# Expert layers: lists for the tokens in two rounds, and half of the results summed in the loop

## The reference

```python
x = x + attn_a(layernorm(x))   # differential attention, 16 heads
x = x + ffn(layernorm(x))      # experts, first time
x = x + attn_b(layernorm(x))   # attention with decay, a scan over the sequence
x = x + ffn(layernorm(x))      # experts, second time
```

```python
scores = softmax(xf @ router_w.T)
topk_scores, topk_ids = top_k(scores, 2)
topk_scores = topk_scores / topk_scores.sum(-1, keepdims=True)
for each expert e:
    h = silu(xf @ w_gate[e]) * (xf @ w_up[e])     # 128 -> 512
    out += weight_of_e * (h @ w_down[e])          # 512 -> 128
```

## Time and profile before

| | us |
|---|---|
| median of 3 runs (1086.36 to 1089.39) | 1087.95 |
| span of the profiled execution | 1143.6 |
| PE busy in it | 992.5 (87%) |
| PEld busy | 675.0 (59%) |
| DVE busy | 751.2 (66%) |
| ACT busy | 744.4 (65%) |
| POOL busy | 438.1 (38%) |

### The profile page before, as it was taken

How to read it: one execution, slowest core, us unless ns; L and a number is a source line. 1 busy time by engine, 2 the same in 40 slices (tenths; PEclk the granted TensorE clock), 3 DMA queues, 4 the chain that set the end, 5 groups by cost and what they waited for, 6 DMA issues and landing times. The chain is left out here.

```text
span 1143.6 us, 27230 instructions
## 1 busy us (share of the span) xinstructions
PE 992.5 (87%) x10390; PEld 675.0 (59%) x10390; DVE 751.2 (66%) x1507; ACT 744.4 (65%) x1507; POOL 438.1 (38%) x580
## 2 busy tenths in 40 slices
PE   5889999999999989747888978999999997688883
PEld 3333333333333335637888866878878876587883
DVE  6789999999999988872222265676666666422223
ACT  4658888888888877344444457767777765544443
POOL 3742112211222111325555334555555542455541
PEclk9879999999999999869999989999999999699997
DMA  2333111111111100611113122202114310211113
GB/s 70 96 114 98 30 32 52 34 30 30 36 52 30 30 2 2 221 44 38 38 37 110 30 75 98 75 38 75 76 75 149 111 39 2 63 38 36 38 34 124
DMA packets 42150, 68.67 MB, mean 60 GB/s; under 512 B 10088, under 2 KB 21096, under 8 KB 40104
## 3 DMA queue, kind: packets, MB, share of 16 engines
q1 hardware_dynamic: 33848, 54.07, 14.4%
q0 software_dynamic: 4992, 10.23, 3.2%
q10 hardware_dynamic: 3184, 2.63, 0.7%
HBM read 51.79 MB, written 14.68 MB: 58 GB/s over the span
## 5 line engine op out<-in xcount | busy, mean ns | idle before, releaser
L803 ACT ACTIVATE PB<-S 128x512 f32<-128x512 f32 x576 | 307.9, 597 | 71.6 <-PE S L609 66.8
L915 DVE TENSOR_REDUCE mx<-S 128x2 f32<-128x1024 f32 (+1 forms) x192 | 207.6, 1128 | 8.6 <-PE S L595 8.6
L871 POOL TENSOR_SCALAR_AFFINE_SELECT PB<-PB 128x512 f32<-128x512 f32 x128 | 79.0, 635 | 307.2 <-ACT PB L803 307.1
L1452 DVE TENSOR_TENSOR m_hs<-m_gs,m_UP 128x512 f32<-128x512 f32 x78 | 53.7, 688 | 213.2 <-ACT m_gs L1322 171.7
L644 PE MATMUL PV<-PB,VP 128*32 128x256 f32 (+2 forms) x2432 | 177.7, 379 | 0.0
L609 PE MATMUL S<-W 50*128 50x512 bf16 (+3 forms) x768 | 123.9, 328 | 4.9 <-ACT PB L803 4.2
L1250 PE MATMUL m_GP<-m_xt,m_wgu 128*128 128x128 f32 x624 | 89.3, 288 | 42.0 <-ACT m_xt L1318 38.7
L1197 POOL DMA_INDIRECT yd_rows<-m_ys,m_target x78 | 76.7, 983 | 115.5 <-DVE m_ys L1459 106.5
L1318 ACT ACTIVATE m_xt<-m_XT 128x128 f32<-128x128 f32 x78 | 21.6, 277 | 147.0 <-PE m_XT L1241 74.3
L1250 PEld LDWEIGHTS m_GP<-m_xt,m_wgu 128*128 128x128 f32 x624 | 79.7, 200 | 47.4 <-issue 47.4
L595 PE MATMUL S<-W 48*128 48x512 bf16 (+3 forms) x640 | 94.5, 326 | 13.6 <-DVE mx L911 4.9
(11 more groups left out here) (344 smaller groups left out, 1879.2 us busy)
## 6 DMA issues: line engine op xcount, KB each, us to landing
d_LQ<-l_rows SPq DMA_DIRECT2D x15, 1024.0 KB, 4.9
W<-qk_parts SPq DMA_DIRECT2D x210, 32.0 KB
qk_parts<-OT SPq DMA_DIRECT2D x24, 256.0 KB, 3.0
W<-qk_parts SPq DMA_DIRECT2D x30, 96.0 KB
W<-in_L_ffn_w_gate SPq DMA_DIRECT2D x1, 2048.0 KB, 9.4
W<-in_L_ffn_w_up SPq DMA_DIRECT2D x1, 2048.0 KB, 14.4
xn_rows<-m_XN SPq DMA_DIRECT2D x8, 256.0 KB, 2.3
W<-in_L_ffn_w_gate SPq DMA_DIRECT2D x2, 1024.0 KB, 5.4
```

The lines of the kernel that those rows point to most:

```text
L803: nc.scalar.activation(PB[:, j % NPB, :], S2[:, j % 3, :], ACT.Exp, scale=SC).then_inc(exp_done, 1)
L871: nc.gpsimd.affine_select(out=tri, in_=tri, compare_op=ALU.is_ge, fill=0.0, base=0, pattern=[[0, U], [1, P]], channel_multiplier=-1).then_ ...
L915: nc.vector.reduce_max(mx[:, g % 2, c, :, heads[0], qb], S1[:, b, :, 0:w], AX.X)\
```

## The change

The slots are ordered by sequence. First come the full slots that the first sequence's tokens alone fill, expert by expert, then for each expert a slot with the rest of them, filled up with tokens of the second sequence; these are at most FIRST = 8 * 2 + 7 = 23 slots. What is left of the second sequence follows, in slots by expert again. SLOTS stays 39.

The lists are made in two rounds, one for each sequence's tiles. The first needs two rounds of marks (23 slots wide) in place of four, and eight of its slots are gathered at once (EARLY = 8). The second round's counts stand on PE behind the first's, its bounds on DVE ahead of the slots, and the rest of it between the slots of DVE's queue, behind the gate of slot s and in front of the copy of slot s - 1. PE's products of the second round, 16 matmuls, stand behind the down matmuls of slot 3. POOL gathers nothing more until the scatter of slot 4, then two slots a scatter until it is nine ahead. The normalised rows of the second sequence are made on DVE in slot 3. In the first layer, the statistics of eight tiles move behind the first sources.

Once the first 23 slots are scattered, SP fetches the first sequence's results to GA, and DVE adds them, two tiles at a time, in slots 27, 29, 31 and 33; m2 stores these two quarters early. Behind the last slot two quarters are left of four. In m1 the moments of the first two quarters are taken in slots 32 and 36, and the front of `decay_attention` is arranged anew: its first rows need no sums.

RC and IV of the second round have PSUM banks of their own. Of the new functions, `first_bounds` has six linked steps (each waits for the one before), `second_bounds` five, `positions` seven; `mark_places` is one round of marks as before. The diff, cut to its core:

```diff
+def list_products(nc, IV, place_oh, marks, k, start, stop):
+    planes = 3 if k else 2
+    slots = marks.shape[3]
+    for i in range(8):
+        last = nc.tensor.matmul(IV[:, 0:planes * slots].rearrange("p (a s) -> p a s", a=planes), place_oh[:, k, :, i],
+                                marks[:, k, 0:planes, :, i], start=(start and i == 0), stop=(stop and i == 7))
...
+def first_bounds(nc, chain, lists, tmp, RC):
...
+def second_bounds(nc, chain, lists, tmp, RC):
...
+def positions(nc, chain, lists, tmp, RC, base, bound, OH):
...
+def mark_places(nc, chain, tmp, marks, place_oh, slot_no, lane_no, tile_no, iop, k, placed):
...
+def other_experts(nc, chain, lists, sef, early, etab_ready):
+    chain.link(nc.vector.tensor_tensor(sover[:, :, 2 * E:], lists["ios"][:].unsqueeze(2).to_broadcast([1, SLOTS, E]),
+                                       lists["late_ends"][0:1, 1:].unsqueeze(1).to_broadcast([1, SLOTS, E]), ALU.is_ge))
+    chain.link(nc.vector.reduce_sum(sef[:], sover[:], AX.X))
+    for k in (E - 1, 2 * E - 1):
+        chain.link(nc.vector.scalar_tensor_tensor(out=sef[:], in0=sover[:, :, k], scalar=-float(E), in1=sef[:], op0=ALU.mult,
...
+    EARLY = 8
+    FIRST = HT * 2 + E - 1
+    SUMS = FIRST + 4
...
+        def gathers_upto(s):
+            return EARLY if s < 4 else min(EARLY + 1 + 2 * (s - 4), s + 9, SLOTS)
...
             def _(sp):
+                for q in range(2):
+                    rows_out(q, xn_ready, TQ * q + TQ)
+                for q in range(2):
+                    rows_out(2 + q, xn_late, TQ * q + TQ)
+                all_stored(sp, FIRST)
+                for q in range(2):
+                    for k in range(2):
+                        sp.dma_start(GA[:, q, k], result_rows(k, q)).then_inc(first_gathered[q][k], 16)
...
             def _(pool):
+                for s in range(EARLY):
                     gather(s)
                 pool.wait_ge(targeted, 1)
+                issued = EARLY
                 for s in range(SLOTS):
+                    if s == EARLY:
+                        pool.wait_ge(targeted, 2)
                     scatter(s)
+                    if issued == EARLY and gathers_upto(s) > EARLY:
+                        pool.wait_ge(xn_stored[1], 16 * 2)
+                        pool.wait_ge(sourced, 2)
+                    for g in range(issued, gathers_upto(s)):
+                        gather(g)
+                    issued = gathers_upto(s)
...
             def _(pe):
+                first_counts(nc, RCA, route).then_inc(rca_done, 1)
+                second_counts(nc, RCB, route).then_inc(rcb_done, 1)
+                products(IVA, place_a, marks_a, 0)
...
                     down(s, e)
+                    if s == 3:
+                        products(IVB, place_b, marks_b, 2)
...
             def _(dve):
+                for k in (1, 0):
+                    mark_places(nc, chain, tmp, marks_a, place_a, slot_no[:, 0:FIRST], lane_no[:], tile_no[:, 0],
+                                lists["iop"][:, 0:1], k, placed)
...
+                make_sources(nc, chain, lists, token, 0, EARLY, sourced)
+                first_experts(nc, chain, lists, sef, EARLY, etab_ready)
+                if statistics_done < NT:
+                    moments(statistics_done, NT)
+                make_targets(nc, chain, lists, row, empty, 0, EARLY, targeted)
+                if statistics_done < NT:
+                    scale(2, statistics_done, NT, False)
+                    distances()
+                dve.wait_ge(rcb_done, 1)
+                second_bounds(nc, chain, lists, tmp, RCB)
...
                 for s in range(SLOTS):
                     gate(s)
+                    if s == 0:
+                        positions(nc, chain, lists, tmp, RCB, lists["rest"][:], lists["whole"][:], OH[:, :, HT:])
+                    elif s in (1, 2):
+                        marks_of_second(2 - s)
+                    elif s == 3:
+                        late_rows()
+                    elif s == 5:
+                        other_experts(nc, chain, lists, sef, EARLY, etab_ready)
+                    elif s == 6:
+                        make_targets(nc, chain, lists, row, empty, EARLY, SLOTS, targeted)
+                    elif s == 7:
+                        weights()
+                    elif s in range(SUMS, SUMS + HT, 2):
+                        early_sums(s - SUMS)
+                    elif follow is not None and s in (SUMS + TQ + 1, SUMS + HT + 1):
+                        early_moments(s - SUMS - TQ - 1)
                     if s:
                         y_copy(s - 1)
+                    if s == 4:
+                        other_lists()
...
@@ decay_attention, ACT
-                weigh_results(0)
-                weigh_results(1)
+                deviations(slice(0, 2 * TQ), 0)
+                rows(0)
                 weigh_results(2)
...
@@ decay_attention, DVE
+                row_scales(0)
+                row_scales(1)
+                add_results(2)
+                row_moments(2)
+                add_results(3)
+                row_scales(2)
+                row_moments(3)
```

More of the change, by code:

```diff
@@ new lines, in second_bounds @@
+def second_bounds(nc, chain, lists, tmp, RC):
+    E, HT = Router.E, Router.NT // 2
+    n = RC[:, HT * E:(HT + 1) * E]
+    over, late, ends = tmp["over"], lists["late"], lists["late_ends"]
+    chain.link(nc.vector.tensor_tensor(over[:], n.unsqueeze(2).to_broadcast([P, E, 2 * HT]),
+                                       lists["edges"][:, HT:].unsqueeze(1).to_broadcast([P, E, 2 * HT]), ALU.is_gt))
+    chain.link(nc.vector.reduce_sum(late[:, 1:], over[:], AX.X))
+    chain.link(nc.vector.tensor_tensor(late[:, 1:], late[:, 1:], lists["counts"][:, 1], ALU.subtract))
+    chain.link(nc.vector.tensor_tensor_scan(out=ends[:], data0=lists["ones_f"][:, 0:E + 1], data1=late[:], initial=0.0,
+                                            op0=ALU.mult, op1=ALU.add))
+    chain.link(nc.vector.tensor_tensor(lists["jump"][:], ends[:, 0:E], lists["past"][:], ALU.subtract))
@@ L1079, in moe @@
     FK = FF // P
+    HT = NT // 2
     NTOK, ROWS = NT * P, 2 * NT * P
@@ L1111, in moe @@
         wts = sb("wts", [P, 2, NT]) if follow is None else follow["wts"]
[L1112 to L1119, removed]
+        marks_a, marks_b = sb("marks_a", [P, 2, 3, FIRST, 8], BF16), sb("marks_b", [P, 2, 3, SLOTS, 8], BF16)
+        place_a, place_b = (sb(k, [P, 2, P, 8], BF16) for k in ("place_a", "place_b"))
+        sef = sb("sef", [1, SLOTS])
+        token, row, empty = (sb(k, [P, SLOTS]) for k in ("token", "row", "empty"))
+        etab, iv, source, target = (lists[k] for k in ("etab", "iv", "source", "target"))
         xs, xt = sb("xs", [P, XB, P]), sb("xt", [P, 2, P])
@@ L1224, in _ @@
-                counts()
-                order = [c for c in range(PC) if c >= PC // 2] + [c for c in range(PC) if c < PC // 2]
-                for m, c in enumerate(order):
-                    pe.wait_ge(placed, m + 1)
-                    planes = 3 if c >= PC // 2 else 2
-                    for i in range(PI):
-                        last = nc.tensor.matmul(IV[:, 0:planes * SLOTS].rearrange("p (a s) -> p a s", a=planes),
-                                                place_oh[:, c, :, i], marks[:, c, 0:planes, :, i],
-                                                start=(m == 0 and i == 0), stop=(m == PC - 1 and i == PI - 1))
@@ L1442, in _, with late_rows @@
[L1442 to L1447 removed]
+                def late_rows():
+                    for t in range(HT, NT):
+                        nc.vector.tensor_scalar(XN[:, t], X[:, t], mv[:, t, 0:1], rstd[:, t:t + 1], ALU.subtract, ALU.mult)\
+                          .then_inc(xn_late, 1)
```

431 lines of the change are left out of this document (270 added, 161 removed).

## The result

The changed kernel takes 1104.01 us (median of 4 runs, 1103.07 to 1107.59), the kernel before 1088.67 beside it: a ratio of 1.0138, interval 1.0104 to 1.0172. It is slower by 15.3 us, where 4.1 were forecast, and lies 7 us above the range.

A forecast was written before the change was run, and what follows sets the result against it. PE was taken to bound the slots, at a floor of 2.79 us each, holes left out. Slot costs of 17.1 less gains of 13.0 gave +4.1, so the median 1087.95 would become 1092.0 us, range 1080 to 1097.

The forecast's parts named there:

- price of the slots: Both loops over expert slots: inserted work costs 8.3 us per layer, twice 16.6, with the first layer's moments 17.1.
- marks: Slots, on DVE: two rounds of marks for the second sequence, 1.40 each, cost 1.3 us per layer.
- products: Slots, on PE: the second round's 16 matmuls cost 1.6 us per layer, bounds 1.43 and 2.87.
- experts and ninth gather: Slots: the other experts on DVE cost 1.4 us, the ninth gather behind the fifth scatter 0.8, per layer.
- early sums: Late slots, on DVE: four pairs of sums, each 1.2 us with a wait, cost 4 x 0.45 = 1.8 per layer.
- moments: First layer's slots, on DVE: 1.25 us twice, one between slots already delayed, cost 0.5.
- Holes, half or all: Rivals: timed loops have holes hiding half of DVE's price (1086.0 us, chance 0.28) or all (1079.8, chance 0.17).
- First front: Ahead of the first layer's slots: -1.6 us, limited by ACT's order; bounds -1.0 and -4.1.
- Second front: Ahead of the second layer's slots: fewer rounds of marks give -3.4 us, from -2.8 to -3.9.
- The decay attention: Its front: sums and moments of two quarters done beforehand, last quarter transposed earlier, -4.1 us, from -3 to -5.
- POOL held by DVE: Rival, slots: DVE's new work delays POOL's transfers, 1096.2 us; chance 0.10, shared with slot 27 late.
- The signs: Changed kernel: first gather at 11 to 13 us, later weights' copy, keys within 5, two tail quarters, PE waits in named slots.

The follow-up runs named there:

- third experiment: Changed kernel with the copies and multiplications in the first bounds written as two-input DVE operations; 1098.73 us, ratio 1.0102.
- fourth experiment: Changed kernel with the early sums one tile to a slot, slots 27 to 34, first-layer moments in slots 35 and 37; 1100.14 us, ratio 1.0103.
- first experiment: Changed kernel with DVE's copy of the slot before right behind the gate, the inserted work behind that copy; 1085.53 us, ratio 0.9958.
- second profile of before: The kernel before, unchanged, profiled once more; one time of 1088.79 us, loops 104.93 and 104.90.
- first recording: The kernel before, unchanged, in the profile the prediction read; span 1143.6 us with 54.2 us of holes in its two loops.

## Why the prediction was wrong

The direction was right, the bound too: PE in the slots, and the holes were rightly left out. The step that failed is the price of the slots, 17.1 where 28.2 were measured: products and early sums were priced too low, the delay of the ninth gather behind the experts too, and a fall of the clock was put at nothing. Against the steps of before (2.57 at first, 2.79, 1.95 at last), term by term:

| per layer, us | predicted | first layer | second layer |
|---|---|---|---|
| marks | 1.3 | 1.4 | 1.2 |
| late rows | 1.4 | 1.45 | 1.45 |
| products | 1.6 | 2.9 | 2.85 |
| clock behind them | 0 | 1.6 | 0 |
| experts and ninth gather | 2.2 | 3.3 | 3.25 |
| early sums | 1.8 | 3.4 | 4.2 |
| moments | 0.5 | 0.9 | - |

- **Products.** I named both ends, 1.43 and 2.87, and took 1.6, by the slot's own matmuls. It is the other end. In the kernel before, the sixteen of 117 columns took 3.44 at a granted clock of 0.50, and the sixteen of 78 behind them 2.56 (line L1231 by window again):

```profile
978.34:980.90 2.56, 2.53 (x17) 2.16 (x15) 0.50 0.00 0
```

So eight and eight are 3.00 at 0.50 (not 2.87: the narrow ones are not faster in proportion), and they took 3.04 and 3.02 at 1.00. Their pace comes from the spaced operand and not from the clock; with adjacent columns 1.12 are left. The Trainium skill ("SBUF — State Buffer", section "Door 1: The DMA port swizzle") states a penalty for each access that goes to a new 16-byte line; the 1.9 us between the two layouts agree. The fall of the clock behind the products (1.6) wasn't in the sum at all. It is not in every execution: the same products in the profiles of the third and fourth experiment had none behind them.
- **Sums.** The work was rightly sized (1.26 for four products), and I counted what exceeds a slack of 0.75. A stop costs PE 0.3 more here than it lasts, and the slack is smaller, 0.64: 0.54 late where 0.45 was counted. 0.86 in place of 0.45, four times in each layer. In the second layer two of these steps had 0.3 and 0.5 more beside a store of the output; no run separates that.
- **Experts and ninth gather.** DVE's experts (0.47, 1.12, 0.50, 0.17) held the copy, for which PE stood 1.47, thereby the fifth scatter, and behind it the ninth gather; I priced the two links singly. Placed behind the copy, 1.34 and 1.24 are left, and one slot earlier nothing.
- **Marks**: right by luck. I set 0.65 for each of two rounds. The first made a step of 4.21 and 4.06, 1.4 and 1.3 too long: in the first layer PE got its copy 0.96 late and paid 1.43. The second cost 0.06 and 0.07 (steps of 2.85 and 2.86), since behind the stop DVE is ahead of PE: its copy at 524.37 is done before the down matmuls at 525.58. **Late rows**: right. **Moments**: 0.9 for 0.5, all of it in slot 36; those between delayed slots cost nothing, as I had it.
- What I took as given in each of these terms was that the work stands ahead of the copy. That was true of the diff, and so a right premise for the time; but the profile had it in one line that it need not: DVE idle 1.90 in front of each gate. The first experiment shows this place to be worth 15.5 of the 28.2, or some more, since its profile has one fall of the clock more.

**What was gained.** Tail: -3.9 for -3.9. First front: -1.8 for -1.6, by the order on ACT that was named (the weights' copy, from 510.83 on, stands ahead of the transpose's copy, for which PE waits 2.03). Second front: -2.6 for -3.4; the stall of the third experiment, 0.9 by its first gate, is the difference (a slip is small beside it: four rounds of 1.40 less two of 1.15 are 3.30, not 3.35). The decay attention: more than -4.1. Its first keys and last quarter, in the changed kernel, whose stage begins at 648.87, and then in the second profile of before, where it begins at 630.14:

```profile
653.54 1.95 PE L1849 MATMUL d_PA<-d_WK,d_xc 128*128 128x512 f32 x4 [0.50 <-POOL d_xc L2300]
...
662.57 0.60 PE L1897 MATMUL d_AT<-ident,W 128*128 128x128 f32 x4
```

```profile
642.54 3.75 PE L1609 MATMUL d_PA<-d_WK,d_xc 128*128 128x512 f32 x4 [0.28 <-POOL d_xc L2063]
...
651.70 0.60 PE L1657 MATMUL d_AT<-ident,W 128*128 128x128 f32 x4
```

The keys came 4.7 behind the start, as predicted (4.8), the last quarter 13.7 (predicted 15.2), where before had 21.6 and, in its first recording, 19.3. Here PE stays at full clock (granted 1.00, keys 1.95); before it stood, fell to 1.2 GHz (0.50 from 640 to 646 in the second profile) and took 3.38 to 3.75 for them. I took the lengths of before's rows for the stage after.

**Rivals.** Holes, half or all: none, by the second profile. POOL held by DVE: the gathers' median is 0.969 us, where it was 0.968. The Trainium skill ("SBUF — State Buffer", section "SBUF: two separate sides") has the lock for both directions, whoever starts first. The trace agrees for the other one, DVE behind POOL, where I hadn't looked for it: 1.80 for a copy of eight columns, 0.17 in the third experiment.

**The signs.** First gather at 11.1, the weights' copy of the first layer later (15.8 behind the start of its stage, 14.1 before), two quarters in the tail, down matmuls waiting for the copy in slots 1, 3 and 5 and in 27, 29, 31 and 33, a transpose waiting for the ninth gather (0.61): all seen. They showed the mechanisms, and none of them their size.

## What to carry to other kernels

Work put into the slack of an in-order queue has a place as well as a size: look for the operation that another engine waits for, put the work behind it, where the queue is idle until its next input, and not ahead of it. Price a stop of a pipelined engine above its length, by a row in which it restarts. For an operand read with a step, take the price from a row with that step and don't scale it with the clock; if PE has to work on it in a full loop, lay it out with adjacent columns.

## What was not expected of the hardware

- A DVE copy with one input from SBUF waited until POOL's 1.93 us constant was written (1.80 for 0.17); the same values by a two-input operation didn't.
- Eight matmuls of 117 and eight of 78 columns, 16 bytes apart, took 3.0 at a granted clock of 1.00; at 0.50 half of sixteen and sixteen (3.44 and 2.56) is 3.0 too. With adjacent columns they took 1.12 at 1.00.
- The granted clock fell to 1.2 GHz right behind such matmuls in 5 of 12 layers, in four of them with PE busy for 8.00 of 8.00 us ahead of the matmuls, and behind none of 6 with adjacent columns.
- One recording of a kernel can have 54 us of holes that neither its timed runs nor a second recording have.
